# A graph network on one core: two PSUM buffers for the spread rows, another order of TensorE's step, turned one-hots on ScalarE, and low one-hots with the tile innermost

## What is computed

```python
# layer 0: 8 heads of 32 features, with an encoding of 3 edge features
h = (x @ W.T).reshape(n, 8, 32);  h_src, h_dst = h[src], h[dst]
enc   = relu(edge_attr @ edge_W.T + edge_b).reshape(-1, 8, 32)
alpha = (h_src*a_src).sum(-1) + (h_dst*a_dst).sum(-1) + (enc*h_dst).sum(-1)
alpha = where(alpha >= 0, alpha, 0.2*alpha)
ex    = exp(alpha - segment_max(alpha, dst)[dst])
attn  = ex / max(segment_sum(ex, dst)[dst], 1e-10)
out   = segment_sum(h_src * attn[..., None], dst) + bias
x = layernorm(x + out)
# layers 1 to 4: sums of x[src] over the edges of each dst (three means, one normalised sum)
# layers 5, 6: two attention layers with 4 heads
```

## Time and profile before

| | |
|---|---|
| runs | 3377.16, 3378.81, 3385.23 us |
| the profiled execution | 3369.06 us, of which the span is 3367.3 us, granted TensorE clock 0.89 on average |
| busy, whole span | TensorE 80%, its weight loads 50%, VectorE 54%, GpSimd 46%, ScalarE 37% |
| adjacency stage, 54 to 272 us | VectorE busy 209 of 218 us, TensorE 187, ScalarE 145 |
| edge layer, 317 to 985 us | VectorE busy 597 of 668 us, TensorE 583, GpSimd 397, ScalarE 350 |

### The profile page before, as it was taken

One profiled execution on the slowest core, in us unless ns is written; L12 is line 12 of the kernel. 1 busy time (PEld: TensorE's weight loads), 2 busy tenths in 40 slices (PEclk: granted clock), 3 DMA queues, 4 the chain that ended last, 5 costly groups with the idle time before them and its releaser, 6 DMA issues.

```text
span 3367.3 us, 50777 instructions
## 1 busy us (share of the span) xinstructions
PE 2709.2 (80%) x12657; PEld 1684.7 (50%) x12658; DVE 1816.8 (54%) x4825; ACT 1251.8 (37%) x3222; POOL 1534.2 (46%) x1469
## 2 busy tenths in 40 slices
PE   6887888888889999999997998466667856666665
PEld 4444555555555555555555455344545534444443
DVE  7996988988963000000003002466666537666665
ACT  3664555555543001001003003644444455444445
POOL 5931666666624004004004000577777447777760
PEclk8997999999989999999998999687787768888885
DMA  6445777777731331331330432455555335555541
GB/s 220 127 112 148 216 202 198 213 198 198 213 88 48 103 89 49 102 90 48 99 94 20 117 102 58 118 140 139 141 138 142 87 98 138 140 140 141 137 114 39
DMA packets 310911, 421.13 MB, mean 125 GB/s; under 512 B 56707, under 2 KB 245047, under 8 KB 310367
## 3 DMA queue, kind: packets, MB, share of 16 engines
q1 hardware_dynamic: 235679, 231.06, 23.7%
q0 software_dynamic: 60544, 173.03, 19.5%
q10 hardware_dynamic: 14400, 13.93, 1.5%
HBM read 378.03 MB, written 39.84 MB: 124 GB/s over the span
## 4 chain that ended last, share of the span: by engine, by line
PE 46%; POOL 18%; DVE 15%; issue 12%; ACT 3%; DMA 3%; DVEq 1%; SPq 0%; ACTq 0%; POOLq 0%
PE ps L760 24%; POOL rows L2151 18%; PE ps L631 5%; PE ps L610 4%; DVE norm L1530 3%; PE ps L1000 3%; PE ps L980 2%; DVE norm L1353 2%; DVE spread L1520 2%; DMA rows<-table,src_idx 1%; ACT norm L1171 1%; PE ps L920 1%; PE ps L817 1%; PE ps L597 1%; DVE al L1359 1%
## 5 line engine op out<-in xcount | busy, mean ns | idle before, releaser
L2151 POOL DMA_INDIRECT rows<-table,src_idx x1248 | 1320.7, 1058 | 538.4 <-issue 376.6
L760 PE MATMUL ps<-rows,rT 128*128 128x448 f16 x2800 | 764.3, 355 | 20.6 <-DMA rows<-adjacency 13.0
L760 PE MATMUL ps<-rows,spread 128*128 128x448 f16 x1400 | 496.4, 355 | 0.0
L760 PEld LDWEIGHTS ps<-rows,rT 128*128 128x128 bf16 x2800 | 275.2, 98 | 280.6 <-issue 28.0
L1565 DVE TENSOR_TENSOR rows<-ps,norm 128x896 f32<-128x896 f32 x21 | 22.9, 1092 | 635.4 <-PE ps L760 635.4
L2105 POOL CAST rT<-rows 128x1024 bf16<-128x1024 f32 (+1 forms) x28 | 26.6, 950 | 737.3 <-ACT rows L1295 509.1
L817 PE MATMUL ps<-rows,spread 128*128 128x260 f32 x832 | 289.1, 519 | 62.4 <-DVE rows L1676 62.3
L610 PE MATMUL ps<-rT,spread 128*128 128x272 f32 x832 | 251.0, 426 | 69.7 <-DVE norm L1353 67.7
L817 PE MATMUL ps<-rows,w_roots 128*128 128x260 f32 x832 | 254.2, 465 | 43.0 <-DVE rows L1676 43.0
L817 PEld LDWEIGHTS ps<-rows,spread 128*128 128x128 f32 x832 | 215.4, 267 | 119.8 <-DVE rows L1676 64.4
L1676 DVE TENSOR_TENSOR rows<-rows,ps 128x1024 f32<-128x1024 f32 x208 | 249.1, 1198 | 29.2 <-issue 21.6
(11 more groups left out here) (268 smaller groups left out, 4180.6 us busy)
## 6 DMA issues: line engine op xcount, KB each, us to landing
rows<-adjacency SPq DMA_DIRECT2D x140, 560.0 KB, 4.0
rT<-table SPq DMA_DIRECT2D x316, 136.0 KB, 3.1
spread<-in_tiles SPq DMA_DIRECT2D x104, 256.0 KB, 3.8
rows<-table,src_idx POOLq DMA_INDIRECT x1248
rT<-table ACTq DMA_DIRECT2D x100, 136.0 KB
w_table<-in_tiles SPq DMA_DIRECT2D x52, 256.0 KB
adjacency<-rT SPq DMA_DIRECT2D x4, 2800.0 KB, 14.0
adjacency<-acc SPq DMA_DIRECT2D x3, 2800.0 KB, 14.2
```

The source lines that it names most:

```text
L760: ins = mm(chunk_ps[c % 2][:, f, :], xp[k][:, t, f * P:(f + 1) * P], ring[q][:, i, :], start=t == 0 and k == 0, stop=t == ROWS - 1 and k = ...
L2151: pool.indirect_dma_start(src_rows(l, par)[:, k, :], None, tables[l][:, :], bass.IndirectOffsetOnAxis(ap=src_idx[:, g * T + k:g * T + k + ...
```

## The change

- `h_ps` becomes two buffers (banks 0 and 1, banks 2 and 3) of 264 instead of 272 columns for each tile (the eight columns in front of the features are no longer spread). `spread(m, q)` waits for the products two earlier instead of one.
- In exchange `edge_node_ps` and `edge_out_ps` with `edge_den_ps` have one buffer each (bank 6, bank 7), and `turn_sums(g)` waits until the window of g-1 is added, not that of g-2.
- TensorE's step runs: encode 0, spread 0, encode 1, spread 1, encode 2, sums half 0, turn_scores, spread 2, encode 3, spread 3, sums half 1, turn_back, turn_sums, rescales.
- The turned one-hots leave VectorE and are made by ScalarE as relu(1 - |rank - row|): an Abs and a Relu, both of 1024 columns, behind the first and the second half of `hot`.
- The low one-hots lie with the tile innermost: `[128, 128 nodes, 16 tiles]`. They are compared with a table `iota_lo` of the same shape, made once in set-up, so that all operands run with unit step; TensorE reads a tile's weights with a step of sixteen f16, 32 bytes.

```diff
+        iota_lo = sb("iota_lo", [P, P, LO_TILES], F16)
-        lo_hot = [... .rearrange("p (t n) -> p t n", t=LO_TILES)
+        lo_hot = [... .rearrange("p (n t) -> p n t", t=LO_TILES)
-        h_ps = ps[:, 0:2, 0:TW]
+        h_ps = [ps[:, 0:2, 0:TW - 8], ps[:, 2:4, 0:TW - 8]]
-        edge_node_ps = [ps[:, 6 + b, 0:TW] for b in range(2)]
+        edge_node_ps = ps[:, 6, 0:TW]
...
             def spread(m, j, h, q):
-                if not (q == 0 and isinstance(m, int) and m == 0):
-                    pe.wait_ge(prod_ready, 4 * m + q)
+                if not (q < 2 and isinstance(m, int) and m == 0):
+                    pe.wait_ge(prod_ready, 4 * m + q - 1)
-                    ins = mm(ps[:, i, 0:TW], edge_turned[:, par, k, :], spans[:, k, :], start=True, stop=True)
+                    ins = mm(h_ps[q % 2][:, i, :], edge_turned[:, par, k, :], spans[:, k, H:TW], start=True, stop=True)
...
             def turn_sums(g, b):
-                    pe.wait_ge(windows_done, g - 1)
+                    pe.wait_ge(windows_done, g)
...
-                    lo, hot = lo_hot[t // LO_TILES % 2][:, t % LO_TILES, :], key_hot[t % KEY_BUFS]
+                    lo, hot = lo_hot[t // LO_TILES % 2][:, :, t % LO_TILES], key_hot[t % KEY_BUFS]
...
+            def turned_off(x, j, h):
+                act.wait_ge(high_landed[par], 16 * (turn + 1))
+                if not (isinstance(x, int) and x < 2):
+                    act.wait_ge(h_ready, 4 * (x - 1))
+                nc.scalar.activation(edge_turned[...], high_row[:, par, :], ACT.Abs, scale=-1.0,
+                                     bias=rank[:, 0:1]).then_inc(turned_step, 1)
+            def turned_hots(x, j, h):
+                act.wait_ge(turned_step, x + 1)
+                nc.scalar.activation(of_x, of_x, ACT.Relu, scale=-1.0, bias=unit[:, :]).then_inc(edge_turned_ready, 1)
...
-                V.tensor_tensor(lo_hot[b % 2], iota16[:, 0:P].unsqueeze(1).broadcast_to([P, LO_TILES, P]),
-                                lo_of[:, b * LO_TILES:(b + 1) * LO_TILES].unsqueeze(2).broadcast_to([P, LO_TILES, P]),
+                V.tensor_tensor(lo_hot[b % 2], iota_lo[:, :, :],
+                                lo_of[:, b * LO_TILES:(b + 1) * LO_TILES].unsqueeze(1).broadcast_to([P, P, LO_TILES]),
                                 ALU.is_equal).then_inc(lo_made, 1)
...
             V.tensor_copy(iota16[:, :], iota[:, 0:KEYS])
+            V.tensor_copy(iota_lo[:, :, :], iota[:, 0:P].unsqueeze(2).broadcast_to([P, P, LO_TILES]))
```

More of the change, by code:

```diff
@@ L228, in gnn_program @@
         whole = spread[:, 2560 + TILES:2560 + TILES + PACKS].bitcast(I32)
-        lo_hot = [spread[:, b * LO_TILES * P // 2:(b + 1) * LO_TILES * P // 2].bitcast(F16).rearrange("p (t n) -> p t n", t=LO_TILES)
+        lo_hot = [spread[:, b * LO_TILES * P // 2:(b + 1) * LO_TILES * P // 2].bitcast(F16).rearrange("p (n t) -> p n t", t=LO_TILES)
                   for b in range(2)]
@@ L291, in gnn_program @@
         gat_den_ps = [ps[0:4, 2 + b, D:D + P] for b in range(2)]
-        edge_den_ps = [ps[0:9, 2 + b, D:D + P] for b in range(2)]
+        edge_out_ps = ps[:, 7, 0:D]
+        edge_den_ps = ps[0:9, 7, D:D + P]
         den_ps = [ps[:, 6 + b, 0:9 * len(x)].rearrange("p (k h) -> p k h", h=9) for b, x in enumerate(DEN_PARTS)]
@@ L355, in gnn_program @@
         hot_step = sem("hot_step")
+        turned_step = sem("turned_step")
         rescaled = sem("rescaled")
@@ L630, in sum_tiles @@
                 for k in ks:
-                    ins = mm(edge_node_ps[par], edge_hot[par][:, k, :], src_rows(l, b)[:, k, 0:TW],
+                    ins = mm(edge_node_ps, edge_hot[par][:, k, :], src_rows(l, b)[:, k, 0:TW],
                              start=k == 0, stop=k == T - 1)
@@ L670, in step @@
                     encode(*of_m, 1)
+                    spread(*of_m, 1)
+                    encode(*of_m, 2)
                 sums(g, j, 0, range(0, 4))
@@ L674, in step @@
                 if m is not None:
-                    spread(*of_m, 1)
-                    encode(*of_m, 2)
-                if m is not None:
                     spread(*of_m, 2)
                     encode(*of_m, 3)
+                    spread(*of_m, 3)
                 sums(g, j, 1, range(4, 6))
                 sum_tiles(j % 2, j, range(6, 8)).then_inc(node_ready, 1)
-                if m is not None:
-                    spread(*of_m, 3)
                 if n is not None:
@@ L1060, in hot @@
                     nc.scalar.activation(edge_hot[par], edge_hot[par], ACT.Relu, scale=-1.0, bias=unit[:, :]).then_inc(onehot_ready, 1)
+            def turned_off(x, j, h):
+                par, turn = pair_of(j, h)
+                act.wait_ge(high_landed[par], 16 * (turn + 1))
+                if not (isinstance(x, int) and x < 2):
+                    act.wait_ge(h_ready, 4 * (x - 1))
+                nc.scalar.activation(edge_turned[:, par, :, :].rearrange("p t e -> p (t e)"), high_row[:, par, :], ACT.Abs, scale=-1.0,
+                                     bias=rank[:, 0:1]).then_inc(turned_step, 1)
+            def turned_hots(x, j, h):
+                par, turn = pair_of(j, h)
+                act.wait_ge(turned_step, x + 1)
+                of_x = edge_turned[:, par, :, :].rearrange("p t e -> p (t e)")
+                nc.scalar.activation(of_x, of_x, ACT.Relu, scale=-1.0, bias=unit[:, :]).then_inc(edge_turned_ready, 1)
             def encoded(m, q):
@@ L1098, in step @@
                 b = (j + 1) % SUM_BUFS
+                of_x = None if m is None or is_last(m) else (m + 1, *next_group(j, h, 3))
                 if m is not None:
@@ L1104, in step @@
                     hot(n, b % 2, 0)
+                if of_x is not None:
+                    turned_off(*of_x)
                 if m is not None:
@@ L1108, in step @@
                     hot(n, b % 2, 1)
+                if of_x is not None:
+                    turned_hots(*of_x)
                 if m is not None:
@@ L1117, in edge_act @@
             nc.scalar.activation(enc.rearrange("p b t (h d) -> p (b t h) d", h=H)[:, :, 0:1], unit[:, :].unsqueeze(2).broadcast_to([P, 4 * H, 1]), ACT.Copy)
+            turned_off(0, 0, 0)
+            turned_hots(0, 0, 0)
             for q in range(4):
                 encoded(0, q)
+            turned_off(1, 1, 0)
+            turned_hots(1, 1, 0)
             hot(0, 0, 0)
@@ L1123, in edge_act @@
                 encoded(1, q)
+            turned_off(2, 2, 0)
+            turned_hots(2, 2, 0)
             weights(0, 0)
@@ L1457, in step @@
                 m = None if n is None or is_last(n) else n + 1
-                of_n, of_x = next_group(j, h, 1), next_group(j, h, 3)
+                of_n = next_group(j, h, 1)
                 messages(g, j, 0)
-                if m is not None and not is_last(m):
-                    turned_hots(m + 1, *of_x)
                 if not (isinstance(g, int) and g == 0):
```

26 lines of the change are left out of this document (9 added, 17 removed).

## The result

The changed kernel took 3403.3 us, median of five runs (3399.24 to 3406.03), against 3377.16 of the kernel before in the same session (five runs). The ratio is 1.0083, 95% interval 1.0069 to 1.0097: slower by 0.8%. The forecast was 3382, "no change", with a range of 3332 to 3407: the time lies in the range, 21 us above the forecast. Rivals C (3401) and D (3404) gave nearly this number too, so the number alone tells little and the trace has to decide.

The account below looks back on a forecast made before the run. VectorE, with TensorE close, was taken to bound the adjacency stage, and order within a step the edge layer. -20 and +23.5 made +3.5 on the profiled 3369.06 us, 3382 on the median's scale; range 3332 to 3407.

Parts of the forecast that it names:

- Rival C: Edge layer: idle pieces bring the lower clock into 25 of 50 steps instead of 14, giving 3401 us; chance 0.14.
- D: Adjacency stage: the layout change does nothing, low one-hots stay at 2.28 us, giving 3404 us; chance 0.06.
- The adjacency stage, -20: Adjacency stage with set-up: -25.4 from faster low one-hots, +1.8 set-up copy, +4 hitches; -20 us, bounds -26 and -12.
- the set-up copy: VectorE's set-up before the adjacency stage: the copy making iota_lo, with nothing over it, adds 1.8 us.
- the new round: Adjacency stage: a round, one batch of low one-hots to the next, takes about 7 us instead of 8.02.
- E: Adjacency stage: weight loads with a 32-byte step become TensorE's limit, +73 us there, giving 3477 us; chance 0.05.
- 163 against 96 ns: TensorE's weight loads: 24-byte step against contiguous, taken as a cache-line penalty; still under a matmul's 0.21 us, costed at 0.
- The loop of the edge layer, 12.87: Edge layer: a step from encode 0 to encode 0 takes 12.87 us against 12.40, +23.5 us over 50 steps.
- rival B: Edge layer: last_spans doesn't hold encode 2, a step takes 11.9 us, giving 3334 us; chance 0.17.
- The turned one-hots on ScalarE, 0: Edge layer: ScalarE's added 2.3 us a step lies beside TensorE's loop with about 0.5 to spare, costing nothing.
- The clock: Edge layer: the granted clock, 0.96 on average, was taken to cost no change, bounds -15 and +20 us.
- rival A: Whole kernel: the forecast itself, 3382 us, spanning 3363 to 3396; chance 0.58.

Follow-up runs that it names:

- run 1: The kernel before with only the new tile-innermost layout of the low one-hots: 3356.43 us, ratio 0.9946.
- run 5: The changed kernel with two extra matmuls per step, their result unread, filling TensorE's idle tail: 3370.04 us, ratio 0.9979.
- Run 10: The changed kernel with the tail filled by two unread matmuls and ScalarE's last_spans loads issued a step ahead: 3354.18 us, ratio 0.9944.
- run 2: The changed kernel with spread 3 moved back behind the second half of the sums: 3405.29 us, ratio 1.0087.
- run 7: The changed kernel with the turned one-hots made on VectorE again: 3404.71 us, ratio 1.0093.
- runs 4 and 6: The changed kernel with TensorE's step in the order of before: 3364.29 us; the same with the turned one-hots back on VectorE: 3336.57 us.
- run 3: The changed kernel with encode 2 moved behind turn_scores: 3358.55 us, ratio 0.9955.
- run 8: The changed kernel with encode 2 behind turn_scores and the turned one-hots on VectorE again: 3346.53 us, ratio 0.9909.
- run 6: The changed kernel with TensorE's step in the order of before and the turned one-hots on VectorE again: 3336.57 us, ratio 0.9878.

## Why the prediction was right and where it was wrong

**The adjacency stage, -20: right.** -18.9 in the trace, -18 by run 1. The low one-hots (1.22 forecast, 1.217), the delay by the set-up copy (1.8 forecast, 1.70) and the new round (6.96 forecast, 6.95 the median) came as worked out. Where TensorE holds VectorE some rounds are longer, up to 7.5. The weight loads stayed hidden, at 144 ns for a 32-byte step, so rivals D and E are out. But the prediction read the earlier trace rows wrongly: its 163 against 96 ns compares a row at the lower clock with one at the full. At the full clock a 32-byte step costs 144 against 96; at the lower one 151, 163 and 167 ns stand for contiguous, 24 and 32 bytes. The Trainium skill's page "Advanced Engine Details and Errata" (section "SBUF Cachelines") has a penalty for going to another line at each access. The trace agrees in that the 32-byte step costs 48 ns at the full clock; of the 67 ns that the prediction took for such a penalty, 163 less 96, most is the lower clock.

**The loop of the edge layer, 12.87: right to 0.1.** It is read where the clock doesn't disturb it, in run 5. Encode 0 to the sums: 626.78 - 622.88 = 3.90, forecast 0.49 + 2.47 + 0.98 = 3.94. Turn_scores to spread 3: 630.56 - 628.72 = 1.84, forecast 0.38 + 1.45 = 1.83. The halves of the sums 1.94 and 1.84, forecast 2.03. Spread 3 0.96, forecast 1.0. The tail 635.63 - 633.36 = 2.27, forecast 2.09. In all 12.75, and over the 43 steps of run 5 at full clock the median is 12.78. Run 10 shows that `last_spans` was the holder of encode 2, as said, so rival B is out.

One thing the list of terms passed over: a second path, from the scans through VectorE's maxima to turn_back, is as long. It shows as the 0.40 wait at turn_back in the changed kernel, and it is why run 2 brought nothing.

**The turned one-hots on ScalarE, 0: right for this order** (run 7), and it was said that they would be paid without their cover. In the old order they are: 28 us between runs 4 and 6.

**The clock, "I take no change, bounds -15 and +20": the step that failed.** Rival C had the mechanism, the place (the bare tail) and the sign. The change itself cost 28 us by the clock, as worked out below, where I had put the most likely value at 0 and the upper bound at 20. I had taken shorter single gaps for a reason that the clock would hold; what the rows show is that the stretch behind the tail runs at 0.50 although no gap in that tail is over 0.55 us. The Trainium skill ("TensorE: Matmul & The Clock Gate", section "A second HAM failure mode: psum-queue depth-cycling") tells of a kernel in which short idle times between groups of matmuls, often enough, made the clock swing between its two levels; the trace agrees, with 0.40 and 0.55 us in each tail and 0.87 over the layer. C foresaw 25 such steps instead of 14; they are 42 instead of 16. Each is cheaper than the 1.7 us I had, which was right for the kernel before (14.07 - 12.41 = 1.66 between the medians): now it is 13.61 - 12.77 = 0.84, since a part of the slow stretch falls on spread 1 and encode 1, behind which encode 2 would have waited for ScalarE anyway.

The idle tail is not all that counts. With encode 2 moved and nothing put into the tail, the clock rose as well, from 0.87 to 0.91 (run 3) and to 0.94 (run 8 against run 7); how the waits ahead of the sums take part in that is open.

The traces give the sum. From the first turn_scores of the layer to the last, the 51 steps take 665 us before, 712 in the changed kernel and 676 in run 5. 51 steps at the medians of full clock (12.41, 12.77 and 12.78) would be 633, 651 and 652, so 32, 61 and 25 us are left for the lower clock and for uneven steps. The loop thus cost 18 us more than before, and the rest, the lower clock in the main, 28 more; the 33 of run 5 is larger because the filling also took away some 7 us that the kernel before loses as well. With the adjacency stage at -18 the sum is -18 + 18 + 28 = +28, against 26 between the medians.

That the time fell into the range is no sign that the sum was right: the forecast itself, rival A, ended at 3396, and 3403 lies in the range only because it was drawn to take in C and D as well.

**What each part of the change is worth**, by runs that differ in it alone: the layout -18 (run 1); two buffers, with what came with them, -20 (run 6 against run 1); the new order +68 with the one-hots on VectorE (run 7 against run 6, 3404.7 against 3336.6), with the clock at 0.87 against 0.94. Of the 68, 58 are the place of encode 2 alone (run 7 against run 8); the one-hots on ScalarE 0 in the new order, +28 in the old one. Two gains of 18 and 20 us were made and paid for by an order that didn't need to change.

## What to carry to other kernels

When an order is changed, walk the loop once more with every engine that takes part, and look at what the moved instruction now waits for: here encode 2 went ahead of half the sums and took a wait on ScalarE, which had always been there, into TensorE's path. Price the clock by the stretch, not by the longest gap: here a tail of small matmuls with gaps of 0.4 and 0.55 us was followed by 1.2 GHz in most steps, and two matmuls in each step whose result nobody reads were worth 33 us. Before two rows are compared, look at the granted clock of both. And try the parts of a change one by one: here the sum hid two gains.

## What was not expected of the hardware

- The granted clock fell behind a stretch with the tail in it, in which TensorE was busy for 2.56 of 3.5 us with no gap over 0.55 us; with 3.23 of 3.40 us busy in the same place it stayed at 1.00, also over a wait of 0.71 right behind it (run 5).
- Filling the tail added nothing to a step at full clock: the median is 12.78 us with the two extra matmuls (run 5, 43 steps) and 12.77 without them (the changed kernel, nine steps).
- Weight loads of 128 columns of 16 bits take 96 ns contiguous and 144 with a step of 32 bytes at a granted clock of 1.00, and 151 and 167 at 0.50; the 163 of the earlier trace rows for 24 bytes were all taken at 0.50.
